# Six transformer layers on one Trainium2 core: values on 32-row tiles of TensorE, q and k rotated before they are scaled, exponentials per head, in a new order

## The reference

```
def attn_layer(x, Wqkv, qs, ksc, Wo):          # 16 heads of 64 channels, window 32
    q, k, v = split(x @ Wqkv); q = l2norm(q) * qs; k = l2norm(k) * ksc
    q = q * cos * scale + rotate_half(q) * sin * scale
    k = k * cos * inv + rotate_half(k) * sin * inv
    out = local_attention(q, k, v)             # a window of 32 queries sees itself and the 32 keys before
    return out.reshape(b, n, INNER) @ Wo
def ffn_layer(x, g, bln, W1, b1, W2, b2):      # layer norm, 341 hidden channels, exact gelu gate
    a, gate = split(norm(x) @ W1 + b1)
    return a * gelu(gate) @ W2 + b2
```

## Time and profile before

| | |
|---|---|
| median of three runs | 2561.2 us |
| profiled execution, and its span | 2554.95 us, 2553.1 us |
| mean granted TensorE clock | 0.954 of 2.4 GHz |
| part B starts near | 785 us |
| busy share of the span: PE, DVE, ACT, POOL | 89%, 86%, 79%, 52% |

### The profile page before, as it was taken

The page is one execution under the profiler, slowest core; times in us unless marked ns, Lnnn a source line. Parts: engine busy times, 40 slices in busy tenths (PEclk is TensorE's granted clock), DMA queues, the critical chain, the costliest instruction groups (busy, mean ns, idle before and its releaser), DMA issues.

```text
span 2553.1 us, 65940 instructions
## 1 busy us (share of the span) xinstructions
PE 2267.3 (89%) x27383; PEld 1361.1 (53%) x27383; DVE 2192.4 (86%) x2513; ACT 2022.9 (79%) x3616; POOL 1322.4 (52%) x894
## 2 busy tenths in 40 slices
PE   5899999999995788999999899999999999999886
PEld 3122222222223566766776666766666667766664
DVE  6999999999854988989899888889888889988873
ACT  1288777888784688888888888888988889889773
POOL 4111111101003667777777777777776777777650
PEclk8699999999997899999999999999999999999987
DMA  1223222222111100101001100101010100110000
GB/s 38 75 59 92 59 79 70 82 51 64 34 63 47 32 21 10 58 18 26 9 10 60 34 9 10 60 16 26 10 60 16 26 8 10 59 30 19 20 14 17
DMA packets 115166, 95.83 MB, mean 38 GB/s; under 512 B 72118, under 2 KB 89780, under 8 KB 114868
## 3 DMA queue, kind: packets, MB, share of 16 engines
q1 hardware_dynamic: 114516, 91.42, 12.9%
q10 hardware_dynamic: 352, 0.20, 0.1%
HBM read 57.83 MB, written 27.26 MB: 33 GB/s over the span
## 4 chain that ended last, share of the span: by engine, by line
PE 46%; DVE 25%; ACT 19%; issue 9%; POOL 0%; DMA 0%; DVEq 0%; ACTq 0%; SPq 0%; POOLq 0%
PE O_ps L1264 10%; PE E_ps L1256 9%; DVE ss L967 7%; PE B_ps L1367 6%; PE S_ps L1247 5%; DVE mx L923 4%; PE B_ps L1288 4%; PE B_ps L1290 3%; PE B_ps L1289 3%; ACT nrm L686 3%; DVE rs L974 3%; ACT pT L755 2%; ACT pT L753 2%; PE B_ps L1354 2%; DVE tc L1005 2%
## 5 line engine op out<-in xcount | busy, mean ns | idle before, releaser
L670 ACT ACTIVATE PT<-E_ps 128x512 f32<-128x512 f32 x1024 | 534.3, 602 | 186.6 <-PE E_ps L1256 184.9
L923 DVE TENSOR_REDUCE mx<-S_ps 128x1 f32<-128x1024 f32 x512 | 601.3, 1218 | 31.0 <-PE S_ps L1247 25.4
L612 POOL TENSOR_TENSOR tc<-tc,ts 128x1024 f32<-128x1024 f32 x96 | 229.2, 2387 | 240.3 <-DVE ts L1017 240.3
L1247 PE MATMUL S_ps<-KS,QS 48*128 48x512 bf16 x1024 | 326.7, 403 | 30.1 <-DVE mx L923 22.1
L1256 PE MATMUL E_ps<-QS,KS 64*128 64x512 bf16 x1024 | 318.0, 387 | 4.7 <-ACT PT L670 4.6
L548 POOL CAST w_cut_b<-w_raw_b 128x512 fp32r<-128x512 f32 (+1 forms) x48 | 27.6, 574 | 550.7 <-DMA w_raw_b<-in_Wqkv 413.5
L570 POOL TENSOR_TENSOR pr<-pr,mxB 128x1024 f32<-128x1024 f32 x96 | 182.8, 1904 | 241.0 <-DVE mxB L1056 241.0
L1288 PE MATMUL B_ps<-w_qkv,x_cut 128*128 128x512 f32 x576 | 263.5, 457 | 33.0 <-issue 16.6
L967 DVE TENSOR_REDUCE ss<-nrm 128x16 f32<-128x1024 f32 x192 | 227.9, 1215 | 69.4 <-ACT nrm L686 69.3
L1264 PE MATMUL O_ps<-PT,va 128*32 128x512 f32 x2048 | 278.3, 616 | 0.0
L1314 PE MATMUL B_ps<-ident,tc 128*128 128x128 f32 x1536 | 216.2, 290 | 64.1 <-ACT o_T L727 56.3
(11 more groups left out here) (199 smaller groups left out, 4679.4 us busy)
## 6 DMA issues: line engine op xcount, KB each, us to landing
Wqkv_cut<-w_cut_b SPq DMA_DIRECT2D x72, 256.0 KB, 2.4
w_qkv<-Wqkv_cut SPq DMA_DIRECT2D x36, 512.0 KB, 5.6
rot<-in_rot SPq DMA_DIRECT2D x96, 128.0 KB, 2.5
w_raw_b<-in_Wqkv SPq DMA_DIRECT2D x36, 256.0 KB, 3.0
W_cut<-w_cut_b SPq DMA_DIRECT2D x24, 170.5 KB, 2.7
w<-W_cut SPq DMA_DIRECT2D x12, 341.0 KB
QS<-zp_q SPq DMA_DIRECT2D x96, 32.0 KB
w_o<-in_Wo SPq DMA_DIRECT2D x6, 512.0 KB, 4.2
```

Source lines behind the costliest of these rows:

```text
L670: e.activation(m.PT[n % NPT][:, :], turns.bank("probs", n)[:, :], ACT.Exp).then_inc(turns.sem("probs", n), 1)
L923: e.tensor_reduce(m.mx[h % 2][:, i, hf:hf + 1], m.S_ps[n % 2][:, :, :], AX.XY, ALU.max).then_inc(s["sc_max"], 1)
L1247: mm = e.matmul(m.S_ps[n % 2][:, c, :], m.QS[sl][rows, i * P:(i + 1) * P], m.KS[sl][rows, k:k + CH], start=True, stop=True)
```

## The change

- **Values.** `diagonals`, `pT` and `pL` are gone. A copy of v shifted down by 32 tokens, `vs`, is made by two DMAs for each tile (`shift_v`, 384 KB and 128 KB, issued by SyncE two turns after the projection). TensorE then makes 128 products for each tile, each with 32 rows and 64 columns of weights and 32 moving columns. Four tiles of the array take turns (two row groups, which write to different banks, times two column groups); half way TensorE waits on a semaphore of its own. One copy of 128x1024 takes the values out.
- **Rotation.** VectorE rotates both q and k out of PSUM, before they are normalised. GpSimd adds the parts of each, does the refinement of the root with three small operations, and multiplies q and k by it.
- **Exponentials.** VectorE makes minus eight times the maxima (`negated`). ScalarE makes 16 exponentials of 128x64, one for each head, out of PSUM with that as bias and with the row sum as second output. The subtraction and the sum of VectorE are gone. The bank of the scores is free when the exponentials are done.
- **Output.** One product group of 128 columns for each tile in place of 256 for each pair.
- **Order, banks, offsets.** All five loops and `BANKS` are rewritten; the loop is two turns longer.

```diff
-FIRST, LAST = 0, END + 12
+FIRST, LAST = 0, END + 14
-BANKS = {"q": ((0, 1), (0, 1)), "k": ((2, 3), (2, 3)), "v": ((6, 7), (6, 7)),
...
+BANKS = {"q": ((4, 5), (4, 5)), "k": ((2, 3), (2, 3)), "v": ((6, 7), (6, 7)),
+         "q_turn0": ((7,), (1,)), "q_turn1": ((6,), (6,)), "k_turn0": ((1,), (1,)),
+         "k_turn1": ((0,), (0,)), "values": ((6, 7), (6, 7)), "output": ((7,), (6,)),
+         "score": ((0, 1), (0, 1)), "mean": ((7,), (7,)), "var": ((4,), (4,)),
+         "up0": ((0, 1), (0, 1)), "up1": ((6, 7), (6, 7)), "up2": ((4, 5), (4, 5)),
...
+    def shift_v(u):
+        w.wait_ge(s["v_out"], u + 1)
+        w.wait_ge(s["pv_mm"], u - 1)
+        to, have, tail = m.vs[u % 2], m.v[u % NV], m.v[max(u - 1, 0) % NV]
+        e.dma_start(to[WIN:P, :], have[0:P - WIN, :]).then_inc(s[f"shift{u % 2}"], 16)
+        e.dma_start(to[0:WIN, :], tail[P - WIN:P, :]).then_inc(s[f"shift{u % 2}"], 16)
...
     def exponentials(u):
-        e.activation(pb[:, :, :], pb[:, :, :], ACT.Exp, scale=8.0).then_inc(s["smexp"], 1)
+        for h in range(H):
+            a = e.activation(pb[:, h, :], sc[:, h, :], ACT.Exp, bias=m.mxB[:, 3, h:h + 1], scale=8.0,
+                             accum_out=m.mxB[:, 1, h:h + 1])
+        a.then_inc(s["smexp"], 1)
...
+    def values(u):
+        bank = banks.two("values", u).rearrange("p a (j b i) -> p a j b i", b=2, i=WIN)
+        w.wait_ge(s["pT"], u + 1)
+        w.wait_ge(s["v_out"], u + 1)
+        w.wait_ge(s[f"shift{u % 2}"], 32 * (u // 2 + 1))
+        banks.wait_free(w, "values", u)
+        for b in range(2):
+            for j in range(NP):
+                for k, v in enumerate((m.v[u % NV], m.vs[u % 2])):
+                    for par in range(2):
+                        for a in range(2):
...
+                                mm = e.matmul(bank[at, a, j, b, :], v[r, d:d + DH], m.pc[u % 2][r, par * NP + j, keys],
+                                              start=(b == j == k == 0), stop=True, skip_group_check=True)
+            if b == 0:
+                mm.then_inc(s["pv_half"], 1)
+                w.wait_ge(s["pv_half"], u + 1)
...
@@ vector_b, the loop, the part for tiles @@
+        square_sums(tile(u - 1), 1)
+        root_argument(tile(u - 1))
+        rotate_cos(tile(u - 1), 1)
+        maxima(tile(u - 2))
+        negated(tile(u - 2))
+        rotate_sin(tile(u - 1), 1)
+        residual_1(tile(u - 3))
+        prob_reciprocals(tile(u - 2))
+        rotate_cos(tile(u), 0)
+        rotate_sin(tile(u), 0)
+        square_sums(tile(u), 0)
+        blocks(tile(u - 2))
@@ tensor_b, the loop @@
+        score(tile(u - 2))
+        values(tile(u - 3))
+        project(tile(u), 0)
+        down_product(chunk(u - 9))
+        finish(late(u - 10))
+        output(tile(u - 3))
+        project(tile(u), 1)
+        mean(chunk(u - 3))
+        dense_output(early(u - 2))
+        turn(tile(u - 1), 0, 0)
+        turn(tile(u - 1), 0, 1)
+        turn(tile(u - 1), 1, 1)
+        turn(tile(u - 1), 1, 0)
+        project(tile(u), 2)
+        up_product(chunk(u - 6), 0)
+        up_product(chunk(u - 6), 1)
+        up_product(chunk(u - 6), 2)
+        variance(chunk(u - 4))
```

More of the change, by code:

```diff
@@ L101, in tile @@
     return x if 0 <= x < END else None
-def pair(x):
-    return (x - 1) // 2 if x % 2 and 0 <= x < END else None
 def chunk(x):
@@ L146, in bank_users @@
     for u in range(FIRST, LAST):
[L147 to L153 removed]
+        take("score", tile(u - 2))
+        take("values", tile(u - 3))
+        take("q", tile(u))
+        take("down", chunk(u - 9))
+        take("finish", late(u - 10))
+        take("output", tile(u - 3))
+        take("k", tile(u))
+        take("mean", chunk(u - 3))
+        take("att", early(u - 2))
+        take("q_turn0", tile(u - 1))
+        take("q_turn1", tile(u - 1))
+        take("k_turn1", tile(u - 1))
+        take("k_turn0", tile(u - 1))
+        take("v", tile(u))
         take("up0", chunk(u - 6))
         take("up1", chunk(u - 6))
[L156 to L159 removed]
         take("up2", chunk(u - 6))
[L161 to L165 removed]
+        take("var", chunk(u - 4))
     return users
@@ L485, in sync_b @@
     load_mlp(0)
-    for x in range(1, END + 11):
+    for x in range(1, END + 13):
         if x < END:
@@ L1425, in tensor_b @@
     for u in range(FIRST, LAST):
-        values(tile(u - 4), 1)
-        dense_output(early(u - 4))
-        turn(tile(u - 2), 0, 1)
-        turn(tile(u - 2), 0, 0)
-        turn(tile(u - 2), 1, 0)
-        turn(tile(u - 2), 1, 1)
-        project(tile(u - 1), 2)
+        score(tile(u - 2))
[12 more added lines that the diff above has]
+        project(tile(u), 2)
         up_product(chunk(u - 6), 0)
         up_product(chunk(u - 6), 1)
-        down_product(chunk(u - 7))
-        variance(chunk(u - 5))
-        finish(late(u - 8))
-        output(pair(u - 4))
         up_product(chunk(u - 6), 2)
-        score(tile(u - 2))
-        project(tile(u), 0)
-        mean(chunk(u - 4))
-        project(tile(u), 1)
-        values(tile(u - 3), 0)
+        variance(chunk(u - 4))
 def build(nc, d, out):
```

371 lines of the change are left out of this document (139 added, 232 removed).

## The result

The changed kernel takes **3024.2 us** (median of 4 runs, 3014.4 to 3028.3) against 2559.5 of the kernel before on the same chip (4 runs, 2557.5 to 2571.7): ratio **1.180**, 95% interval 1.177 to 1.183. It is 465 us slower, where 2601 was forecast and 2745 was the end of the range. Of the runs further down, e10, e12 and e15 have one slow execution each, which the medians in the table hold and the ratios leave out.

The account below looks back on a forecast made before the run. It took the kernel to be bound by how three engines hand work to each other, each turn 16.2 us: 2555 + 50 for part B's chunks - 10 at the end = 2595, plus 6 for the median, 2601 us; range 2470 to 2745.

Parts of the forecast that it names:

- the rings: Cycles of engines waiting on each other within a part B turn, said to set its length: 16.2 us, +2.1 a chunk.
- V: TensorE's time for a tile's values, 128 products or 256 records: 4.3 us in place of 3.21, bounds 3.6 and 7.7.
- 66.5 us a chunk: TensorE's summed work on four tiles in the changed kernel, below the 71.2 us the forecast gave a chunk.
- Which no ring includes: Sign of being wrong: the granted TensorE clock falling below 0.95 in the middle of the run.
- Rival 4: Weight loads of the values take turns at 27 ns a record: V 7.7, +13.6 us a chunk, 2927 us; chance 0.06.
- cheap exponentials: Rival with ScalarE's exponentials at 0.22 to 0.25 us each, turn 14.9 us: 2489 us; chance 0.37.
- E = 4.8: ScalarE's time for a tile's 16 exponentials with row sums, taken at 0.30 us each: 4.8 us.
- The rings 10.9 + E and 11.4 + E: Turn length: 10.9 + E us at least, through scores, values, ScalarE's copies and squares; 11.4 + E, 16.2 us, taken.
- the second ring: Cycle closed by VectorE, from squares of q through rotation, maxima and negation to the exponentials: 9.9 to 12.9 + E us.
- The negation: VectorE's new small operation on the maxima ahead of the exponentials, expected between 0.2 and 1.7 us.
- Rival 5: ScalarE's load falls by 5 us but its free time only moves to waiting for the values: 2601 us.
- The tail, -10: End of the kernel after the last copy of v, 83 us before: allowed to shorten by 10 us, bounds 0 and 25.

Follow-up runs that it names:

- e10: Changed kernel in a spread order with 80 values products (transposed probabilities shifted by DMA), q and k projections both between scores and values: 2795 us, ratio 1.087 to 1.093.
- e12: Changed kernel in a newly planned order of all engines, with 80 values products a tile and transposed probabilities shifted by DMA: 2781 us, ratio 1.077 to 1.090.
- e15: e12 with the down product and what follows it two turns earlier: 2699 us, ratio 1.045 to 1.053.
- e14: Changed kernel with every operation kept, in a newly planned order of all engines, with the down product two turns earlier: 2640 us, ratio 1.026 to 1.032.
- e3: Changed kernel with every values product moving 64 columns of probabilities instead of 32, same number of instructions: 3013 us, single execution.
- e7: Changed kernel with VectorE's subtraction, one wide exponential and VectorE's row sums back in place of the negation and 16 exponentials: 3017 us, single execution.
- e5: Kernel before the change with the 64 score products of a tile issued twice (256 further instructions): 2861 us, single execution.
- e13: e12 with the projection of k issued twice (12 more dense instructions a turn): 2763 us, ratio 1.074 to 1.081.
- e16: e15 with the projection of k issued twice (1.4 us more dense TensorE work a turn): 2688 us, ratio 1.044 to 1.051.

## Why the prediction was wrong

- **Sign right, size far off.** Slower had 0.51. The forecast's 40 us came from the rings; the 465 came from two things that no term of the sum held. So the sign was right by luck.
- **What failed** is the cost V of the values and the clock, put at its upper level throughout, and with both the path. The measured pieces put into the prediction's own sum for TensorE, 66.5 us a chunk, give 66.5 + 4 x (3.85 for the values + 1.2 for q + 1.1 for the output) = 91 us, an estimate with the pace of q and the output taken from the one turn shown. Measured is 90.3. No ring is needed to explain it.
- **V = 4.3 for the values** failed as a cost in its place: 8.5 in the turn shown, 8.15 in the mean. It was worked out from the pace of the tail products, 16 records that need no new block, by which 256 records (and their 256 loads) in a row were priced. As work it was right: 4.4 in a turn of e14, though at 14.6 ns a record where 13.5 was taken, with less beside it than the 0.8 us allowed. What it left out is 2.8 us of pauses and 1.4 us of a second half at the lower clock.
- **"Which no ring includes"**: the prediction named a granted clock under 0.95 as a sign that it was wrong, and put the term at nothing. It fell to 0.82, with up to 355 of the 465 us. q and the output were carried over at 1.5 and 1.84 us and took 2.7 and 3.0.
- **Rival 4** (V 7.7, 2927, chance 0.06) came nearest in its numbers and not in its mechanism. The loads of weights do not take turns at 27 ns: the records run at 14.5 to 16 ns, at 27 to 28 only at the lower clock, and e3 shows that twice the columns are free. That "it alone outweighs even cheap exponentials from V 5.1" was right.
- **The floor of 25 ns** between two matmuls of the Trainium skill's page "TensorE: Matmul & The Clock Gate" (section "Wait — 56ns, not 53.3ns?"): records start 14.5 to 16 ns apart here. The trace disagrees, unless two records of a float32 product count as one (29 to 32 ns).
- **E = 4.8**: 4.62 measured, 0.29 from head to head. The row sum is an instruction of its own, whose start overlaps the exponential:

```profile
1516.63 1.02 ACT L722 ACTIVATE o_T<-B_ps 128x1024 f32<-128x1024 f32 x1 [6.13 <-PE B_ps L1307]
1517.55 0.31 ACT L733 ACTIVATE pr<-B_ps,mxB 128x64 f32<-128x64 f32 x1
1517.75 0.20 ACT L733 ACTIVATION_READ_ACCUMULATOR pr<-B_ps,mxB 128x1 f32 x1
1517.84 0.32 ACT L733 ACTIVATE pr<-B_ps,mxB 128x64 f32<-128x64 f32 x1
```

- **The rings 10.9 + E and 11.4 + E**: 16.2 was the forecast for a turn, with TensorE waiting in each for the exponentials or the copies of k. It waits for neither, and e7 takes 3.6 us out of E and changes 0.2%. TensorE's own turn, 20 us with its pauses and its slow clock, had grown past them. (The terms listed for the second ring add up to 9.75, not 9.9; nothing hangs on it.) The prediction checked TensorE's work (66.5 a chunk) against the rings at the upper clock only.
- **The negation** at 0.2 to 1.7 us: 174 to 1643 ns, median 1316. Right. The clamp has become fast, 181 to 182.

```profile
L1005 DVE TENSOR_SCALAR mxB<-mxB x53: 174/1316/1643, 1216.5 to 2395.5; 128x16 f32<-128x16 f32 x53
```

- **ScalarE waits ahead of the copy of the values**: right, 606 us in all. **v by DMA costs nothing**: right, nothing waits for `vs`. **Rival 5**, that ScalarE's saving turns into waiting for the values, is what its 63% shows, though with TensorE as the reason.
- **The tail, -10**: the last copy of v starts 91 us before the end in place of 83 (2935.3 of 3026.5): 8 us longer, where 10 shorter was allowed. A small miss.

## What to carry to other kernels

Count the instructions of TensorE as well as its columns: a float32 product of a small tile is four (two passes, each with its load), and where more than some 250 followed one another in under 4 us here, the engine stood still for the next block, with nothing else to wait for. Put large products between them; an order that does so, with the orders of ScalarE and VectorE planned for it, took 384 of these 465 us back (e14) with no operation changed. And price a stretch at the lower clock as a term of its own: of TensorE's time at the lower level in part B 392 us lie in the values and 442 behind them, most of it in projections and output.

## What the runs showed of the hardware

- TensorE's instructions come in packets of 16 KB, 254 records each. A packet is seen about 2.5 us (2.3 to 2.8) before the block's first instruction runs at the pauses of the values, and one fetch in ten follows the one before in less than 3.5 us; 256 small instructions run in 1.5 to 2.1.
- The fetch does not run far ahead: the packet of the next block is seen 1.15 us (median) after a pause of the values ends. In e5 large products stand ahead of the scores in each turn, and still 1.94 us of pause a tile follow.
- With more dense work the granted clock was 0.930 in place of 0.871 and 0.954 in place of 0.897, and the time did not rise (e13, e16). Pauses of 186 us in e5 cost the clock little (0.939).
- 64 columns in a small float32 product take the time of 32: a record starts each 14.6 ns in both (e3).
